# Decoder of two layers on one core: the quantised feed-forward spread over VectorE, ScalarE and GpSimd with four-slot rings, and one TensorE loop placed on a 256-slot boundary

## The reference, cut to what matters

```python
x = x + _L0_ffn_ref(_layernorm(x, axis=-1), clip_x, clip_down, w_gate, w_up, w_down)

scale = sigmoid(clip_factor) * max(abs(x)) / 127            # one number for all tokens
x_q   = clip(round(x / scale), -128, 127) * scale           # activations, 128 channels
h     = silu(x_q @ w_gate.T) * (x_q @ w_up.T)               # 352 hidden channels
h_q   = clip(round(h / scale_h), -128, 127) * scale_h       # same rule, scale from max(abs(h))
y     = h_q @ w_down.T
```

## Time and profile before

| what | value |
|---|---|
| median of three executions | 2507.98 us |
| the profiled execution, its own time | 2510.14 us |
| span of its instructions | 2508.3 us (1.8 us lie around it) |
| mean granted TensorE clock | 0.948 of full |
| PE busy | 2190.0 us, 87% |
| PEld busy | 1802.9 us, 72% |
| DVE busy | 1960.5 us, 78% |
| ACT busy | 1448.3 us, 58% |
| POOL busy | 1216.1 us, 48% |

### The profile page before, as it was taken

The page is one execution under the profiler, slowest core; times in us unless marked ns, Lnnn a source line. Parts: engine busy times, 40 slices in busy tenths (PEclk is TensorE's granted clock), DMA queues, the critical chain, the costliest instruction groups (busy, mean ns, idle before and its releaser), DMA issues. The chain is left out here.

```text
span 2508.3 us, 90125 instructions
## 1 busy us (share of the span) xinstructions
PE 2190.0 (87%) x33097; PEld 1802.9 (72%) x33103; DVE 1960.5 (78%) x5517; ACT 1448.3 (58%) x3893; POOL 1216.1 (48%) x1198
## 2 busy tenths in 40 slices
PE   7999999977777752237999989999999999999998
PEld 7888888865555541136888768887788888888886
DVE  3888888868999978897888667775777777777775
ACT  1666666646666642346888768886444444444443
POOL 0333333327777752008999789996222323222232
PEclk9999999989999986758999989999999999999999
DMA  4000000000000000000000000000000000000000
GB/s 120 3 0 0 0 0 0 0 7 21 17 17 17 17 8 0 0 25 11 0 0 0 1 2 0 0 0 4 8 12 14 10 13 10 10 13 10 13 10 14
DMA packets 56941, 25.64 MB, mean 10 GB/s; under 512 B 18115, under 2 KB 56326, under 8 KB 56838
## 3 DMA queue, kind: packets, MB, share of 16 engines
q1 hardware_dynamic: 53426, 23.06, 3.4%
q10 hardware_dynamic: 3412, 1.19, 0.2%
HBM read 20.04 MB, written 4.19 MB: 10 GB/s over the span
## 5 line engine op out<-in xcount | busy, mean ns | idle before, releaser
L704 POOL TENSOR_TENSOR sa_sc<-sa_sc,sa_rs 128x1024 f32<-128x1024 f32 x64 | 121.9, 1904 | 316.0 <-DVE sa_rs L680 316.0
L1820 POOL TENSOR_TENSOR lo_qk_r<-lo_qk_ms,w_neg_half 128x20 f32<-128x20 f32 x64 | 226.9, 3545 | 22.0 <-DVE lo_qk_ms L1743 21.9
L1820 POOL TENSOR_TENSOR gl_qk_r<-gl_qk_ms,w_neg_half 128x20 f32<-128x20 f32 x64 | 226.6, 3541 | 1.4 <-DVE gl_qk_ms L1743 1.4
L484 POOL TENSOR_TENSOR xan_ve<-xan_mv,w_eps_ln 128x1 f32<-128x1 f32 x64 | 12.1, 189 | 399.6 <-DVE xan_mv L478 399.6
L890 ACT ACTIVATE xa_cT<-xa_misc 128x128 f32<-128x128 f32 x64 | 17.8, 278 | 303.8 <-PE xa_misc L791 274.0
L1014 POOL TENSOR_TENSOR xa_sc<-xa_sc,xa_rs 128x1024 f32<-128x1024 f32 x64 | 121.7, 1901 | 118.5 <-DVE xa_rs L974 118.5
L819 PEld LDWEIGHTS xa_qs<-xan_xT,late_x_wq 128*128 128x128 f32 x1024 | 119.3, 192 | 52.8 <-issue 52.8
L556 PE MATMUL sa_qs<-san_xT,w_a_wq 128*128 128x128 f32 x1024 | 132.0, 283 | 2.6 <-DVE sa_sc L666 2.2
L971 DVE TENSOR_REDUCE xa_sm<-xa_sc 128x16 f32<-128x1024 f32 x64 | 78.1, 1220 | 69.7 <-ACT xa_sc L914 69.7
L819 PE MATMUL xa_qs<-xan_xT,late_x_wq 128*128 128x128 f32 x1024 | 131.4, 282 | 0.0
L830 PE MATMUL xa_pp<-xa_cT,late_x_wk 128*128 128x128 f32 x1024 | 131.1, 281 | 0.0
(11 more groups left out here) (328 smaller groups left out, 6859.6 us busy)
## 6 DMA issues: line engine op xcount, KB each, us to landing
w_x<-in_x_dram SPq DMA_DIRECT2D x8, 512.0 KB, 7.6
ca_cx<-in_ctx_dram SPq DMA_DIRECT2D x64, 64.0 KB, 1.8
xa_cx<-in_ctx_dram SPq DMA_DIRECT2D x64, 64.0 KB, 1.8
out_dram<-xa_out SPq DMA_DIRECT2D x64, 64.0 KB, 1.6
ca_mask<-in_mask_BxSxS_ff_dram SPq DMA_DIRECT2D x64, 32.0 KB, 1.7
w_a_wq<-in_L_attn_Wq_dram SPq DMA_DIRECT2D x1, 512.0 KB
w_a_wo<-in_L_attn_Wout_dram SPq DMA_DIRECT2D x1, 512.0 KB
prep_xwo<-in_L_xattn_Wo_dram ACTq DMA_DIRECT2D x1, 512.0 KB
```

The lines of the kernel that those rows point to most:

```text
L704: pool.tensor_tensor(v, v, bcast(rs[:, s, :], 2, S), ALU.mult).then_inc(prob_done, 1)
L1820: pool.tensor_tensor(qk_r[:, s, :], qk_ms[:, s, :], k["neg_half"][:, 0:NQK], ALU.pow).then_inc(sg["qk_r"], 1)
```

## The change

It has two parts. All of it lies in `ffn`, except an argument of `skewed`.

Rings have four slots where they had two (`normed`, statistics, `up_xr`, `up_xq`, `dn_hr`), and every loop of `ffn` holds four steps. The work of a group is divided anew. In stage A, ACT writes H as scale times x plus offset (4 instructions), DVE makes the offset and the largest magnitude of every group, so that the last reduction reads 16 columns. In stage B, ACT scales and rounds (one instruction of 512 columns), POOL clips (one), DVE subtracts MAGIC (`integers`, one), and DVE reduces the hidden values of each group (`largest`, one instruction of 2 x 512 columns and one of 512 columns on 96 partitions). In stage C, ACT scales and rounds (1024 columns, and 512 on 96 partitions), POOL clips the same two pieces, DVE subtracts MAGIC from them.

The other part: in `wide_cross_attention` TensorE's loop is preceded by `addr_align(256, max_nops=0)`, which places the loop's first instruction at a multiple of 256 instruction slots; the padding is jumped over.

The diff, cut to its core; declarations of tiles, and uses of `s % 2` where a ring kept two slots, are left out.

```diff
-def skewed(eng, n, pieces, unroll=2):
+def skewed(eng, n, pieces, unroll=2, whole_blocks=False):
...
+        if whole_blocks:
+            eng.addr_align(256, max_nops=0)
         with eng.Fori(start // unroll, n // unroll) as i:
...
-                                (1, keys), (3, output), (8, turn_back)], 4)
+                                (1, keys), (3, output), (8, turn_back)], 4, whole_blocks=True)
...
+                def apply(g, s):
+                    after(act, offset_done, g)
+                    for n in range(GROUP):
+                        act.activation(tile_of(H, g * GROUP + n), tile_of(X, g * GROUP + n), ACT.Identity,
+                                       bias=offset[:, s, n:n + 1], scale=rstd[:, s, n:n + 1]).then_inc(normed, 1)
+
+                skewed(act, NG, [(2, apply)], 4)
...
+                skewed(act, NG, [(2, apply)], 4)
...
-                def apply(g, s):
+                def offsets(g, s):
                     after(dve, rstd_done, g)
-                    for n in range(GROUP):
-                        t = g * GROUP + n
-                        dve.tensor_scalar(tile_of(H, t), tile_of(X, t), mv[:, s, n, 0:1], rstd[:, s, n:n + 1],
-                                          ALU.subtract, ALU.mult).then_inc(normed, 1)
-
-                dve.memset(amax[:, :], 0.0).then_inc(cleared, 1)
-                skewed(dve, NG, [(2, apply), (0, statistics), (0, mean_variance)])
-                dve.wait_ge(normed, NT)
-                dve.tensor_reduce(top[:, 0:1], H[:, :], AX.X, ALU.max, apply_absolute_value=True).then_inc(top_done, 1)
+                    after(dve, normed, g, 4, per=GROUP)
+                    dve.scalar_tensor_tensor(out=offset[:, s, :], in0=mv[:, s, :, 0], scalar=-1.0, in1=rstd[:, s, :],
+                                             op0=ALU.mult, op1=ALU.mult).then_inc(offset_done, 1)
+
+                def largest(g, s):
+                    after(dve, normed, g, per=GROUP)
+                    cols = slice(g * GW, (g + 1) * GW) if isinstance(g, int) else bass.ds(g * GW, GW)
+                    to = xmax[:, g:g + 1] if isinstance(g, int) else xmax[:, bass.ds(g, 1)]
+                    dve.tensor_reduce(to, H[:, cols], AX.X, ALU.max, apply_absolute_value=True).then_inc(top_done, 1)
+
+                skewed(dve, NG, [(2, offsets), (0, statistics), (4, largest), (0, mean_variance)], 4)
+                dve.wait_ge(top_done, NG)
+                dve.tensor_reduce(top[:, 0:1], xmax[:, :], AX.X, ALU.max).then_inc(top_done, 1)
...
+                pool.memset(amax[:, :, :], 0.0)
+                skewed(pool, NG, [(0, rsqrt)], 4)
+                pool.wait_ge(top_done, NG + 1)
...
-                    def clip_high(g, s):
-                        dve.tensor_scalar(xr[:, s, :], group_of(H, g), sinv[:, 0:1], QMAX, ALU.mult, ALU.min).then_inc(r1, 1)
-
-                    def clip_low(g, s):
-                        after(dve, r1, g)
-                        dve.tensor_scalar(xr[:, s, :], xr[:, s, :], -QMAX - 1.0, MAGIC, ALU.max, ALU.add).then_inc(r2, 1)
-
                     def integers(g, s):
                         after(dve, r2, g)
-                        after(dve, t_psum, g, 2)
+                        after(dve, t_psum, g, 4)
                         dve.tensor_scalar(xq[:, s, :], xr[:, s, :], MAGIC, None, ALU.subtract).then_inc(q_done, 1)
...
-                    skewed(dve, NG, [(3, hidden(0)), (0, clip_high), (3, hidden(1)), (0, clip_low), (3, hidden(2)), (0, integers)])
-                    dve.wait_ge(h_done, 3 * NG)
-                    for c, (f0, fn) in enumerate(FCH):
-                        last = dve.tensor_reduce(amax[0:fn, c:c + 1], HT[0:fn, c, :], AX.X, ALU.max, apply_absolute_value=True)
-                    last.then_inc(top2, 1)
-                    dve.wait_ge(top2, 1)
-                    dve.tensor_reduce(top[:, 1:2], amax[:, :], AX.X, ALU.max).then_inc(top2, 1)
+                    def largest(g, s):
+                        cols = slice(g * GW, (g + 1) * GW) if isinstance(g, int) else bass.ds(g * GW, GW)
+                        at = slice(g, g + 1) if isinstance(g, int) else bass.ds(g, 1)
+                        after(dve, h_done, g, per=3)
+                        dve.tensor_reduce(amax[:, at, 0:2].rearrange("p g c -> p (g c)"), HT[:, 0:2, cols], AX.X, ALU.max, apply_absolute_value=True)
+                        dve.tensor_reduce(amax[0:96, at, 2], HT[0:96, 2, cols], AX.X, ALU.max, apply_absolute_value=True).then_inc(top2, 1)
+
+                    skewed(dve, NG, [(5, hidden(0)), (2, integers), (5, hidden(1)), (5, hidden(2)), (6, largest)], 4)
+                    dve.wait_ge(top2, NG)
+                    dve.tensor_reduce(top[:, 1:2], amax[:, :, :].rearrange("p g c -> p (g c)"), AX.X, ALU.max).then_inc(top2, 1)
...
+                    def clipped(g, s):
+                        after(pool, r1, g)
+                        gate(k, pool)
+                        pool.tensor_scalar(xr[:, s, :], xr[:, s, :], MAGIC + QMAX, MAGIC - QMAX - 1.0, ALU.min, ALU.max).then_inc(r2, 1)
+
+                    skewed(pool, NG, [(1, clipped)], 4)
+                    pool.wait_ge(top2, NG + 1)
...
+                    skewed(pe, NG, [(3, turn), (4, products)], 4)
...
+                    def scaled(g, s):
+                        after(act, q_done, g, 4)
+                        act.activation(xr[:, s, :], group_of(H, g), ACT.Copy, bias=MAGIC, scale=sinv[:, 0:1]).then_inc(r1, 1)
...
+                    skewed(act, NG, [(3, turned), (0, scaled), (4, silu)], 4)
...
-                    def clip_high(g, s):
-                        cols = slice(g * GW, (g + 1) * GW) if isinstance(g, int) else bass.ds(g * GW, GW)
-                        after(dve, q_done, g, 2, per=3)
-                        for c, (f0, fn) in enumerate(FCH):
-                            dve.tensor_scalar(hr[0:fn, s, c, :], HT[0:fn, c, cols], sinv[0:fn, 1:2], QMAX, ALU.mult, ALU.min).then_inc(r1, 1)
-
-                    def clip_low(g, s):
-                        after(dve, r1, g, per=3)
-                        for c, (f0, fn) in enumerate(FCH):
-                            dve.tensor_scalar(hr[0:fn, s, c, :], hr[0:fn, s, c, :], -QMAX - 1.0, MAGIC, ALU.max, ALU.add).then_inc(r2, 1)
+                    def integers(g, s):
+                        after(dve, r2, g, per=2)
+                        after(dve, y_psum, g, 2)
+                        dve.tensor_scalar(hq[:, s % 2, 0:2, :], hr[:, s, 0:2, :], MAGIC, None, ALU.subtract)
+                        dve.tensor_scalar(hq[0:96, s % 2, 2, :], hr[0:96, s, 2, :], MAGIC, None, ALU.subtract).then_inc(q_done, 1)
...
+                    skewed(dve, NG, [(2, integers), (4, scale_down), (4, residual_x)], 4)
...
+                    def scaled(g, s):
+                        cols = slice(g * GW, (g + 1) * GW) if isinstance(g, int) else bass.ds(g * GW, GW)
+                        after(act, q_done, g, 4)
+                        act.activation(hr[:, s, 0:2, :], HT[:, 0:2, cols], ACT.Copy, bias=MAGIC, scale=sinv[:, 1:2])
+                        act.activation(hr[0:96, s, 2, :], HT[0:96, 2, cols], ACT.Copy, bias=MAGIC, scale=sinv[0:96, 1:2]).then_inc(r1, 1)
+                    skewed(act, NG, [(0, scaled)], 4)
+
+                @block.gpsimd
+                def _(pool):
+                    def clipped(g, s):
+                        after(pool, r1, g)
+                        gate(k, pool)
+                        for v in (hr[:, s, 0:2, :], hr[0:96, s, 2, :]):
+                            pool.tensor_scalar(v, v, MAGIC + QMAX, MAGIC - QMAX - 1.0, ALU.min, ALU.max).then_inc(r2, 1)
+                    skewed(pool, NG, [(1, clipped)], 4)
...
+                    skewed(pe, NG, [(3, down)], 4)
```

More of the change, by code:

```diff
@@ L1260, in ffn @@
         identb = sb("identb", [P, P], BF16)
-        amax = sb("amax", [P, 3])
+        amax = sb("amax", [P, NG, 3])
+        xmax = sb("xmax", [P, NG])
+        offset = sb("offset", [P, 4, GROUP])
         top = sb("top", [P, 2])
@@ L1302, in mean_variance @@
                     after(dve, stats_done, g, per=GROUP)
-                    after(dve, normed, g, 2, per=GROUP)
+                    after(dve, normed, g, 4, per=GROUP)
                     gate(k, dve)
@@ L1402, in turn @@
                         for n in range(GROUP):
-                            last = pe.transpose(tp[s][:, n * P:(n + 1) * P], xq[:, s, n * P:(n + 1) * P], identb[:, :])
+                            last = pe.transpose(tp[s % 2][:, n * P:(n + 1) * P], xq[:, s, n * P:(n + 1) * P], identb[:, :])
                         last.then_inc(t_psum, 1)
@@ L1420, in turned @@
                         after(act, u_psum, g, 2, per=3)
-                        act.activation(xqT[:, s, :], tp[s][:, 0:GW], ACT.Copy).then_inc(t_done, 1)
+                        act.activation(xqT[:, s % 2, :], tp[s % 2][:, 0:GW], ACT.Copy).then_inc(t_done, 1)
                     def silu(g, s):
@@ L1459, in residual_x @@
                         after(dve, scaled, g)
```

(14 more changed lines are left out.)

35 lines of the change are left out of this document (15 added, 20 removed).

## The result

The changed kernel took 2485.04 us (median of three executions, 2481.83 to 2486.13) where the kernel before took 2507.98: ratio 0.9906, 95% interval 0.9881 to 0.993. On another chip it took 2481.94 (run 1) against 2508.12, ratio 0.9893 (0.9878 to 0.9908).

What follows compares the result with a forecast made beforehand. DVE was taken to bound the three feed-forward stages, PE the late phase. From 2510.1 us, less 10.6 (A), 4.6 (B) and 3.8 (next phase), plus 7.8 (C): 2498.9, or 2497 against the median 2507.98; range 2483 to 2515.

Steps and rivals of the forecast that it cites:

- Stage A, the steps: Stage A: DVE's step takes 1.96 us, 2.3 in the loop with 0.35 for waits, all means at 31.5 us.
- Stage A, the end: End of stage A: DVE and ACT ready at 36.0 us, POOL's exposed switch last at 39.0; gain 10.6 us.
- The switch, 6 us with bounds 0 and 9.2: POOL's change between kinds of instruction, in all three stages: 6 us each on idle queues.
- The rival with 9.2: Switch costs 9.2 us on idle queues too; three stages start 3.2 us later, 2506 us; chance 0.15.
- Stage B, the first product: Head of stage B: first clip at 6.75 us behind the start, first product at 13.8, against 6.1 before.
- Stage B, the groups: Stage B after the first product: 66.8 us for groups and loop, 3.5 for held `integers`, 0.3 for the last reduction.
- Stage C: First clip at 7.75 us, POOL's clips and DVE's `integers` in turn, 3.2 us a group; 63.0 us, loss 7.8.
- The rival of the residual sum: Stage C: DVE's residual sum also takes turns with POOL, 0.68 us a group, 10.9 in all; 2508 us; chance 0.15.
- The slower rival: Stages B and C: POOL's clips run at the two-input price, 1.04 and 1.90 us; 2520 us; chance 0.12.
- No turn-taking: Stages B and C: clips and `integers` don't hold each other up, 3.5 and 9.6 us less; 2484 us; chance 0.10.
- Behind it: Head of the next phase: no POOL switch needed there any more, gain 3.8 us (0 to 4.0).
- The late loop, 0: TensorE's late loop in the last phase: its new place gains 0 us; entering costs one jump, 0 to 4 us.

Runs made afterwards that it cites:

- run 1: The changed kernel once more, unchanged, on another chip, as the measure for the runs beside it: 2481.94 us, ratio 0.9893 to the kernel before.
- run 11: The changed kernel with stage C as it was before, on its old engines, ring and loops, A and B as changed: 2484.84 us, ratio 0.9906.
- run 7: The changed kernel with each of GpSimd's clips done twice, values unchanged: 2509.17 us, ratio to the kernel before 1.0005.
- run 8: The changed kernel with VectorE's smaller `integers` of stage C (96x512) given to ScalarE: 2477.33 us, ratio 0.9885.
- run 3: The kernel before with only the alignment of TensorE's late loop added: 2508.45 us against 2508.12, ratio 0.9999.
- run 2: The changed kernel without the alignment of TensorE's late loop, so the feed-forward change alone: 2563.95 us, ratio 1.0219 to the kernel before.
- runs 4 and 5: The kernel before with TensorE's late loop begun 104 or 192 slots behind a multiple of 256: 2509.99 us and 2582.18 us, one execution each.
- run 9: The changed kernel with both reductions over partitions moved from GpSimd to small VectorE and TensorE instructions: 2471.40 us, ratio 0.9858.
- run 6: The changed kernel with a one-column element-wise GpSimd instruction behind each reduction, to begin the switch back earlier: 2482.03 us, ratio 0.9892.

## Why the prediction was right, and where it was off

By its own steps:

- **Stage A, the steps.** Forecast 1.96 us, 2.3 in the loop, all means at 31.5 us; measured 1.70 us in the loop (the lines above that answer to the earlier trace rows) and 26.8 us (L1318's last instruction starts at 952.5). This is one of the two mis-sized terms: stage A gives 5.1 of the 12.7 us by which the four stretches beat the forecast, and 4.7 of them are here. The 0.35 for the waits' register work was taken from no row. Inside a block of four steps it isn't there: DVE's neighbours start with an overlap of about 0.08 each (0.86 + 0.67 + 0.37 + 0.13 is 2.03 for 1.70). It is paid once per block, at the loop's edge (the statistics at 943.81 and 945.85 are 2.04 apart).
- **Stage A, the end.** Right: three microseconds of instructions end first (956.95), the switch last (959.80). It took 5.7 us; I took 6. Its exposed end is the 2.85 us behind 956.95.
- **The switch, 6 us with bounds 0 and 9.2.** Right in the main: 5.7, 6.7 and 6.7 us, in other executions up to 7.8 in stage B. The rival with 9.2 is out on idle queues. The loaded row was no accident: in run 11, with the weights' transfer beside it, it took 10.4 us (pair at 1098.2, `rstd` at 1108.63). The Trainium skill's 6 us (GPSIMD Engine Reference, Instruction dispatch) agrees with the switch to the reduction, 5.7 us; the ways back are 0.7 to 1.8 us longer than the page's figure.
- **Stage B, the first product.** Forecast 13.8 us behind the start, measured 13.82. That close a hit is luck: the first clip came at 7.6 us (forecast 6.75), the rest took 6.2 (forecast 7.05), and in five other traces with the same stage B or one that differs only in the doubled clips the product came at 14.2 to 15.4.
- **Stage B, the groups.** From the first product to POOL's reduction I had 66.8 + 3.5 + 0.3 = 70.6 us; it was 65.1. This is the other mis-sized term, 5.5 us. The 3.5 us for clips that hold `integers` were none: L1378 has 408/413/427 ns. The clip starts 0.2 us behind the end of its scaling (1003.91 + 0.72, then 1004.82), when DVE has left its `integers` (1003.88 to 1004.29) for the products, one of whose two inputs is in PSUM. The step is 4.03, not the 4.25 of 3.77 + 0.38 + 0.1.
- **Stage C.** First clip 8.7 us behind the start (forecast 7.75), pace 3.01 us ((1098.1 - 1052.9) / 15, L1469's first and last start; forecast 3.2). But not as put: POOL was busy for 24 of 37 us, DVE for 35.7 (runs 7 and 8). This step had the wrong path, though nearly the right size: I had the pace from clips and `integers` in turn, 3.2 us, with DVE's two other instructions beside the clips. In fact DVE is full, its list takes 2.4 us a group when nothing is held, and holds in every second group bring the mean to 3.0.
- **The rival of the residual sum** had its mechanism right: L1480 takes 1.50 us when it starts behind a clip, 0.69 otherwise. The Trainium skill (SBUF — State Buffer, Who interferes with whom) says that an instruction of VectorE with two SBUF inputs contends with GpSimd's reads; this trace agrees. Its price, 0.68 a group or 10.9 us, was wrong: the sum is held in 3 groups of 16, 1.7 us in all. Elsewhere beside clips it starts first and the clip is the one that waits (beside L1480 at 1083.18, the clip at 1083.42 takes 0.94 us in place of 0.61).
- **The slower rival** needed clips at 1.04 and 1.90 us; they take 0.60 and 1.03, below my 0.65 and 1.15. **No turn-taking** is refuted by run 7, although its time, 2484, was the nearest: the forecast's steps were too long by 12.7 us for other reasons, so that the wrong rival met the time by luck.
- **Behind it.** 3.6 us gained, forecast 3.8.
- **The range.** Its lower bound, 2483, doesn't follow from what it names. A switch near 0 alone (-15) gives 2482, and joined with no turn-taking (-13) 2469. That 2485.04 lies inside says little for the steps: it was brought there by shorter steps in stages A and B, which the range did not reckon with.
- **The late loop, 0.** Right for the edit alone (run 3). Of the 2.1 us that the last phase is shorter, 0.4 lie up to the end of the loop; most of the rest is the clock. In the windows below, first of before, then of the changed kernel, the same stretch behind the loop has a granted clock of 0.75 (some of it at 1.2 GHz) and of 1.00; L876's 16 matmuls take 3.68 and 2.05 us there. PE had been idle in part in both, so I call it chance, and count it no gain. Run 1 bears this out: in this trace of the same changed kernel the 16 matmuls (L878 there) take 3.38 us again.

```profile
2484.00:2490.00 6.00, 4.27 (x79) 4.17 (x80) 3.10 (x8) 2.35 (x4) 2.67 (x3) 0.75 0.02 4
```

```profile
2460.00:2466.00 6.00, 3.85 (x87) 3.36 (x85) 3.84 (x10) 3.02 (x6) 2.59 (x3) 1.00 0.01 3
```

- **What the alignment hides.** I wrote that the changed code would move the loop and left it without a price. It is the largest number of the case, 82 us (run 2). Without the alignment the direction of the forecast would have been wrong, and no row of before shows it, as its loop happened to lie well.
- **What stays open.** No run separates the four-slot rings and four-step loops from the new division of work in stages A and B, so their gain of 15.7 and 10.0 us is that of both together.

## What to carry to other kernels

Before changing code ahead of a long TensorE loop, find how many blocks of 256 instructions it covers: by the count of runs 4 and 5, 1650 records fit into 7 from some starting slots and need 8 from others, and the place of the loop decided over 75 to 82 us here. Look for an engine that changes between kinds of instruction at every full stop: GpSimd's two small reductions, 0.4 us each, cost about 15 us of the stages, and 8 to 10 us in the medians, until each was three small instructions of other engines. Where GpSimd works beside VectorE, add up the instructions that use the shared path (SBUF to SBUF, or two SBUF inputs) on both, and place GpSimd's beside those that read PSUM or reduce.

## What had not been expected of the hardware

- The place of TensorE's loop: badly placed, it makes 9 fetches of 16 KB in each of 12 passes and stalls in two gaps of up to 3.1 us, while at slots 0 and 104 there are none.
- The hold is mutual and goes by who starts first: a clip begun 0.05 us behind an `integers` took 1.55 us in place of 1.03.
- A pair of MODIFY_POOL_CONFIG doesn't by itself say what a switch costs: 0.1 us to the next instruction between element-wise ones (run 9), 5.6 to 5.7 us towards the reduction, 6.65 to 7.8 back (run 6, with a small `tensor_tensor` as the first one, is no different: 7.4 and 6.8), and 10.4 with the weights coming in beside it (191 GB/s in 1098 to 1109 of run 11).
